# Splitting the second head's weights one stage earlier in a four-layer attention kernel, with the lists of two engines reordered

## What is computed

```python
def _cross_attention(q_in, kv_in, wq, bq, wk, bk, wv, bv, wo, bo, bias_k, bias_v):
    qh = (q_in @ wq + bq).reshape(b, q_len, H, K)      # H, K = 16, 128
    kh = (kv_in @ wk + bk).reshape(b, t, H, K)
    vh = (kv_in @ wv + bv).reshape(b, t, H, K)
    kh = jnp.concatenate([kh, bias_k], axis=1); vh = jnp.concatenate([vh, bias_v], axis=1)
    weights = softmax(einsum('bqhk,bthk->bhqt', qh, kh) / sqrt(K))
    return einsum('bhqt,bthk->bqhk', weights, vh).reshape(b, q_len, H * K) @ wo + bo

x = x + _cross_attention(layer_norm(x, ln1), ctx, ...1)
x = x + _cross_attention(layer_norm(x, ln2), ctx, ...2)
x = x + gelu(layer_norm(x, ln_mlp) @ w_fc1 + b_fc1) @ w_fc2 + b_fc2
```

## Time and profile before

| | |
|---|---|
| median of 3 runs | 1384.41 us (1384.3 to 1389.26) |
| profiled execution | 1390.04 us |
| its span, first to last instruction | 1388.2 us |
| mean granted TensorE clock | 0.93 |
| TensorE busy | 1230.7 us, 89% |
| VectorE, ScalarE, POOL busy | 71%, 52%, 36% |
| opening | 0 to 33.8 us |
| first attention | 33.8 to 353 us |
| norm n02 | 354 to 367 us |
| second attention | 367.6 to 681 us |

### The profile page before, as it was taken

One profiled execution on the slowest core, in us unless ns is written; L12 is line 12 of the kernel. 1 busy time (PEld: TensorE's weight loads), 2 busy tenths in 40 slices (PEclk: granted clock), 3 DMA queues, 4 the chain that ended last, 5 costly groups with the idle time before them and its releaser, 6 DMA issues. The chain is left out here.

```text
span 1388.2 us, 27413 instructions
## 1 busy us (share of the span) xinstructions
PE 1230.7 (89%) x9144; PEld 1014.5 (73%) x9144; DVE 987.8 (71%) x2229; ACT 722.0 (52%) x1636; POOL 495.6 (36%) x642
## 2 busy tenths in 40 slices
PE   5799999999599999999699699969499977699869
PEld 4699999999499999998588455559277756455558
DVE  6478878787578887888763689465488865689464
ACT  4456655666366666566542177441166632177441
POOL 3654545444374445543150000030199940000030
PEclk9899999999799999999899699979799998699979
DMA  4111111010211111010023874020660014874020
GB/s 151 47 31 32 31 30 30 23 30 1 95 32 32 31 31 29 9 38 0 31 65 71 121 83 56 13 77 1 196 131 3 2 51 83 112 81 55 13 65 31
DMA packets 55406, 70.90 MB, mean 51 GB/s; under 512 B 6696, under 2 KB 47404, under 8 KB 52976
## 3 DMA queue, kind: packets, MB, share of 16 engines
q1 hardware_dynamic: 53704, 65.83, 22.8%
q10 hardware_dynamic: 1600, 3.76, 0.9%
HBM read 46.79 MB, written 8.13 MB: 40 GB/s over the span
## 5 line engine op out<-in xcount | busy, mean ns | idle before, releaser
L945 ACT ACTIVATE a_prob<-a_s_ps,a_negmax 128x257 f32<-128x257 f32 x256 | 119.2, 477 | 92.9 <-DVE a_negmax L1027 92.9
L2033 DVE TENSOR_REDUCE s_mx<-s_s_ps 128x2 f32<-128x1024 f32 x128 | 151.9, 1211 | 17.9 <-PE s_s_ps L2078 17.6
L2018 ACT ACTIVATE s_probT<-s_st_ps 128x512 f32<-128x512 f32 x256 | 132.1, 605 | 58.6 <-PE s_st_ps L2092 56.3
L884 POOL TENSOR_TENSOR x_v_hi<-a_v_sum,x_one 128x512 fp32r<-128x512 f32 x60 | 63.2, 1053 | 248.7 <-DVE a_v_sum L1016 248.7
L1822 POOL TENSOR_SCALAR s_below<-s_masked,s_mx 128x256 f32<-128x256 f32 x256 | 117.8, 480 | 30.5 <-DVE s_mx L1850 29.7
L576 POOL TENSOR_TENSOR rstd<-base,power 128x4 f32<-128x4 f32 x4 | 4.0, 1009 | 335.6 <-DVE base L593 335.6
L1042 DVE TENSOR_TENSOR a_pT_lo<-a_t_ps,a_pT_hi 128x512 fp32r<-128x512 f32 x128 | 88.3, 690 | 37.9 <-ACT a_pT_hi L958 36.2
L1027 DVE TENSOR_REDUCE a_negmax<-a_s_ps 128x2 f32<-128x514 f32 x128 | 87.0, 689 | 35.6 <-PE a_s_ps L1088 35.3
L958 ACT ACTIVATE a_pT_hi<-a_t_ps 128x512 fp32r<-128x512 f32 x128 | 76.7, 600 | 59.5 <-PE a_t_ps L1142 56.1
L1850 DVE CUSTOM_DVE_ANT_0 s_masked<-s_s_ps,l_mask 128x256 f32<-128x256 f32 x256 | 90.7, 421 | 16.6 <-PE s_s_ps L1887 16.6
L1835 ACT ACTIVATE s_probT<-s_st_ps 128x512 f32<-128x512 f32 x128 | 69.9, 596 | 29.1 <-PE s_st_ps L1897 29.0
(11 more groups left out here) (289 smaller groups left out, 4069.0 us busy)
## 6 DMA issues: line engine op xcount, KB each, us to landing
a_wo_raw<-L_xattn_wo SPq DMA_DIRECT2D x16, 256.0 KB, 3.2
x_wqk_raw<-L_xattn_wq SPq DMA_DIRECT2D x31, 128.0 KB, 2.3
x_wqk_raw<-L_xattn_wk SPq DMA_DIRECT2D x31, 128.0 KB, 2.3
x_wv_raw<-L_xattn_wv SPq DMA_DIRECT2D x15, 256.0 KB, 3.0
l_k_st<-k_second SPq DMA_DIRECT2D x12, 256.0 KB, 9.6
l_k_st<-k_stack SPq DMA_DIRECT2D x16, 192.0 KB
l_q_st<-q_stack SPq DMA_DIRECT2D x12, 192.0 KB
x_vbias<-L_xattn_bias_v SPq DMA_DIRECT2D x2, 1024.0 KB, 11.0
```

Source lines behind the costliest of these rows:

```text
L945: nc.scalar.activation(prob[:, n % 2, qt, 0:NK], s_ps[:, n % 2, qt, 0:NK], ACT.Exp, bias=negmax[:, n % 2, qt:qt + 1], accum_out=den[:, n % ...
L2018: nc.scalar.activation(probT[:, third % 2, n // 4, n // 2 % 2, n % 2], st_ps[:, u % 3], ACT.Exp, scale=c.scale).then_inc(z.exp_done, 1)
L2033: nc.vector.tensor_reduce(mx[:, i % 2, qt, a::2], s_ps[:, n % 2], AX.X, ALU.max).then_inc(z.max_done, 1)
```

## The change

The second head's `wqk` (slot 1) and the second pair's `wv` are now loaded and split in the stage ahead of each attention: in the opening and in n02. SP loads them there (in the opening once the low parts of the first weights are made, and in front of `prepare_sync`), ScalarE makes the high parts (`split_high`), POOL the low ones (`split_low`). In the attention the first load and split go, the counts that the others wait for are shifted by one, and in the first pair the load of `wv` is left out; the two rows for the next layer are loaded behind `wo`. Apart from that the lists of the opening and of the norms are put into another order; ScalarE norms tiles 4 and 5 too.

```diff
@@ -222,9 +223,8 @@
                                      ALU.subtract, ALU.mult).then_inc(self.z.normed_dve, 1)
 
     def turn(self, pe, half):
-        if half == 0:
-            pe.wait_ge(self.z.normed_act, 2)
-        pe.wait_ge(self.z.normed_dve, (2, 6)[half])
+        pe.wait_ge(self.z.normed_act, 2 * (half + 1))
+        pe.wait_ge(self.z.normed_dve, 2 * (half + 1))
...
@@ -298,6 +296,10 @@
                                  ).then_inc((z.x_in0, z.x_in1)[half], 16)
                 w.load_first_rows(sp, 1, z.vrows_in)
                 sp.dma_start(mask_i[:], ins["mask_BxS2_ik0"]).then_inc(z.mask_in, 16)
+                sp.wait_ge(z.lo_split, 1)
+                w.load_qk(sp, 1, z.second_qk)
+                sp.wait_ge(z.lo_split, 2)
+                w.load_v(sp, 1, z.second_v)
                 w.prepare_sync(sp, z)
                 sp.wait_ge(z.masked, 2)
                 sp.dma_start(core.maskrow, mask_f[:].bitcast(F32)).then_inc(z.mask_out, 16)
@@ -321,23 +323,30 @@
 
                 weights_high(0)
                 context_high(0)
+                context_high(1)
                 weights_high(1)
-                context_high(1)
                 for t in range(2):
                     norm.normalise_scalar(act, t)
                 act.wait_ge(z.cols_in, 16)
                 front.keys_high(act, 0)
+                act.wait_ge(z.second_qk, 32)
+                w.split_high(act, w.second_parts()[0], z.second_hi)
                 front.values_high(act, 0)
+                for t in range(4, 6):
+                    norm.normalise_scalar(act, t)
                 for n in range(2):
                     norm.high(act, n)
                     norm.flat_early(act, n)
                 front.values_high(act, 1)
                 front.keys_high(act, 1)
                 for n in range(2, 4):
-                    norm.high(act, n)
+                    norm.high(act, n, flat=n - 1)
+                front.values_high(act, 2)
                 queries.high(act, 0)
-                front.values_high(act, 2)
                 front.values_high(act, 3)
+                act.wait_ge(z.second_v, 16)
+                front.wait_values(act)
+                w.split_high(act, w.second_parts()[1], z.second_hi)
                 queries.high(act, 1)
 
             @block.gpsimd
...
-                for j in range(4):
+                front.values_low(pool, 0)
+                pool.wait_ge(z.second_hi, 1)
+                w.split_low(pool, w.second_parts()[0], z.second_lo)
+                for j in range(1, 4):
                     front.values_low(pool, j)
+                pool.wait_ge(z.second_hi, 2)
+                w.split_low(pool, w.second_parts()[1], z.second_lo)
 
             @block.tensor
             def _(pe):
...
                 front.keys(pe, 1)
+                front.values(pe, 2)
                 norm.turn(pe, 1)
-                queries.products(pe, 0)
-                for j in range(2, 4):
-                    front.values(pe, j)
-                queries.products(pe, 1)
+                front.values(pe, 3)
+                for g in range(2):
+                    queries.products(pe, g)
 
...
-        names = LayerNorm.SEMS + Queries.SEMS + ("w_in0", "w_in1", "rows_in", "hi_split", "raw_hi")
+        names = LayerNorm.SEMS + Queries.SEMS + ("w_in0", "w_in1", "rows_in", "hi_split", "raw_hi", "second_qk",
+                                                 "second_v", "second_hi", "second_lo")
         z = type("Semaphores", (), {n: st.sem(n) for n in names})
         norm = LayerNorm(st, core, ahead, scale, offset, factor, z)
         queries = Queries(core, ahead, norm.turned, z) if ahead.has_queries else None
         with nc.Block() as block:
             @block.sync
             def _(sp):
+                if queries:
+                    ahead.load_qk(sp, 1, z.second_qk)
+                    ahead.load_v(sp, 1, z.second_v)
                 ahead.prepare_sync(sp, z)
 
             @block.scalar
             def _(act):
                 for t in range(2):
                     norm.normalise_scalar(act, t)
-                for n in range(2):
-                    norm.high(act, n)
-                    norm.flat_early(act, n)
-                if not queries:
+                norm.high(act, 0)
+                norm.flat_early(act, 0)
+                norm.high(act, 1)
+                for t in range(4, 6):
+                    norm.normalise_scalar(act, t)
+                if queries:
+                    act.wait_ge(z.second_qk, 32)
+                    ahead.split_high(act, ahead.second_parts()[0], z.second_hi)
+                else:
                     ahead.prepare_scalar(act, z, range(1))
-                for n in range(2, 4):
-                    norm.high(act, n)
+                norm.high(act, 2)
+                norm.high(act, 3, flat=2)
                 if queries:
+                    act.wait_ge(z.second_v, 16)
+                    ahead.split_high(act, ahead.second_parts()[1], z.second_hi)
                     for g in range(2):
                         queries.high(act, g)
                 else:
@@ -468,12 +493,15 @@
                 core.clear_used(pool)
                 if queries:
                     ahead.first_key_bias(pool, z)
+                    for n, part in enumerate(ahead.second_parts()):
+                        pool.wait_ge(z.second_hi, n + 1)
+                        ahead.split_low(pool, part, z.second_lo)
                 else:
                     ahead.prepare_pool(pool, z)
 
             @block.vector
             def _(dve):
-                norm.shift(dve, 0)
+                norm.shift(dve, 0, 0)
                 for t in range(2, 4):
                     norm.normalise_vector(dve, t)
                 norm.constants(dve)
...
-                dve.wait_ge(z.rstd_done, 1)
-                for t in range(4, TT):
+                norm.low(dve, 0, early=1)
+                norm.shift(dve, 1, 1)
+                for t in range(6, TT):
                     norm.normalise_vector(dve, t)
-                for n in range(2):
-                    norm.low(dve, n)
-                for n in range(2, 4):
-                    norm.flat_after(dve, n)
-                for n in range(2, 4):
-                    norm.low(dve, n)
+                norm.flat_after(dve, 1, high=2)
+                norm.low(dve, 1, late=1)
+                norm.flat_after(dve, 3)
+                norm.flat_after(dve, 2, high=3)
+                norm.low(dve, 2, late=3)
+                norm.low(dve, 3, late=2)
                 if queries:
                     for g in range(2):
                         queries.low(dve, g)
...
+    def second_parts(self):
+
+        return self.qk_parts(1), self.v_parts()
+
+    def split_high(self, act, part, sem):
+        raw, hi, _ = part
+        self.core.nc.scalar.activation(hi, raw, ACT.Copy).then_inc(sem, 1)
+
+    def split_low(self, pool, part, sem):
+        raw, hi, lo = part
+        self.core.nc.gpsimd.tensor_tensor(lo, raw, hi.bitcast(F32), ALU.subtract).then_inc(sem, 1)
...
+        def qk_split(h):
+
+            return 2 * (h - 1)
+
...
@@ -826,24 +878,22 @@
             @block.sync
             def _(sp):
                 def load_qk(h):
-                    wait(sp, z.wqk_split, 2 * (h - 1))
+                    wait(sp, z.wqk_split, qk_split(h - 1))
                     w.load_qk(sp, h, z.wqk_in)
...
-                load_qk(1)
-                if follows:
-                    w.load_first_rows(sp, i + 1, z.next_in)
 
                 def body(p, vs):
                     for s, h, _, fetch in halves(p):
                         if fetch:
                             load_qk(h + 2)
                         if s == 0:
-                            if fetch:
-                                wait(sp, z.wv_split, 2 * p)
+                            if fetch and not first(p):
+                                wait(sp, z.wv_split, wv_split(p))
                                 w.load_v(sp, p + 1, z.wv_in)
                             wait(sp, z.wo_split, 2 * p)
                             sp.dma_start(wo_raw[:], wo[bass.ds(p * PW, PW), :].rearrange("(h p) n -> p h n", p=P)
                                          ).then_inc(z.wo_in, 16)
+                            if follows and first(p):
+                                w.load_first_rows(sp, i + 1, z.next_in)
                 pairs(sp, body)
 
             @block.gpsimd
...
+                    pool.wait_ge(z.wv_in, 16 * (p - 1))
                     wait(pool, z.turn_done, turns.v_out(p - 1))
                     raw, hi, lo = w.v_parts()
                     nc.gpsimd.tensor_tensor(hi, raw, w.times_one(raw.shape[1]), ALU.mult).then_inc(z.wv_split, 1)
-                    pool.wait_ge(z.wv_split, 2 * p - 1)
...
@@ -893,15 +943,13 @@
                                               src[:, bass.ds(h, 1)].bitcast(F32).broadcast_to([P, B])
                                               ).then_inc(z.kbias, 1)
...
```

(8 more changed lines are left out.)

64 lines of the change are left out of this document (33 added, 31 removed).

## The result

The change runs in 1362.99 us (median of 4 runs, 1361.72 to 1364.52), the kernel before in 1384.36 (4 runs, 1379.56 to 1389.26) on the same chip: ratio 0.9847, 95% interval [0.982, 0.9874], 21.4 us less. The forecast was 1360.8, between 1355 and 1371. Two later series of the same file gave 1362.16, ratio 0.9835 [0.9816, 0.9855], and 1362.67, ratio 0.9844 [0.9821, 0.9868].

What follows compares the result with a forecast made beforehand. TensorE, busy 89% of the span, bounds the kernel; only its waits and slow clock at layer edges can be won. Layer one -11.6, layer two -10.5, opening -1.5, norms 0: -23.6 from 1384.4 gives 1360.8 us, range 1355 to 1371.

Steps and rivals of the forecast that it cites:

- The price of the two waits: Attention starts: TensorE's waits for `x_wqk_lo` and `x_wv_lo` plus half clock cost at most 13.1 us (layer one), 11.0 (layer two).
- 0.5 us in each layer for the chain of unit 0: Attention starts: maximum, exponential, normalisation, transposes of unit 0 covered with nothing to spare; 0.5 us kept back per layer.
- 1 us for the clock in layer one: First attention's start: idle TensorE in the opening may drop the clock, costing 0 to 3 us; 1 taken.
- The opening, -1.5: Opening: reordered lists against added splits give -1.5 us, between +1 and -3.5.
- the list by hand (-2.0): Opening: following the lists with the rows' durations, POOL's last subtraction ends latest, at about 31.4, 2.0 us less than before.
- the port: Opening: POOL's two added subtractions could hold up VectorE through the shared port pair, 0 to 2 x 1.1 us; 0.5 taken.
- The norms, 0: Norm between the layers and the one behind: no change, between +1.5 and -1 together; `h_lo` whole at about 364.
- SP's rows in the norm: Norm between layers: rows land at about 366 behind three added loads, stage's last copy at 367.27; covered by 1 us.
- the clock does not come back: Rival: remaining pauses still pull the clock down, only the waits' 16.3 us are returned, 1368 us; chance 0.17.
- The edit does not do what it says: Rival: late second `x_wqk` load holds ScalarE's opening list, each us past 17 moving the opening; 1379 us; chance 0.05.
- The stages ahead pay: Rival: opening and norm end 3 us later each (port, late rows), gain -16 us, 1368 us; chance 0.08.
- The clock sticks low: Rival: half clock persists from a layer's start, 38 us added per pair of heads, 1398 us; chance 0.03.

Runs made afterwards that it cites:

- lists: The change with head two's and value group one's weights loaded and split in the attention as before, only the new list orders kept: 1384.75 us, ratio 1.0006.
- weights: The kernel before with only the early loads and splits of the weights, lists of opening and norms as before: 1363.19 us, ratio 0.9854.
- v_back: The change with the second values group's early load and split put back into the attention, query and key weights still early: 1371.79 us, ratio 0.9904.
- fill_tail: The change with the norms' old lists and 3 + 8 unread extra TensorE products between and behind the opening's query groups: 1358.13 us (one run).
- change_b: The change unaltered, run in the third series beside the second run of the fastest version: 1362.67 us, ratio 0.9844.
- again: The change unaltered, run once more as the measure for its halves: 1362.16 us, ratio 0.9835.
- both: The change with norms' old lists, a POOL wait for VectorE in the opening, extra products at start, opening's tail, norms, 23 before MLP: 1357.19 us, ratio 0.9801.

## Why the prediction was right, and where it was not

- **The price of the two waits.** Right, in size and in mechanism. Taken from the step between score units, it was 13.1 and 11.0 us; where the clock holds, the units take 6.90 or 6.91 us against the 6.83 worked out, and the gain was 13.05 and 10.9. `lists`, `weights` and `v_back` show that it comes from the early weights, and that each of the two has its share. One reading was loose: the clock did not fall behind the wait of 4.9 us but inside it (1.00 in 38 to 39 us, 0.50 in 39.4 to 40.4; the wait ended at 40.38).
- **0.5 us in each layer for the chain of unit 0.** Too much: head 2 is 6.88 to 6.94 in all eleven executions with both weights early. The chain is covered.
- **1 us for the clock in layer one.** Right in its mechanism. It is 1.5 us or nothing from one execution to the next; the row of after shows it (0.50 in 32 to 34 us), and `fill_tail` makes the idle tail its likely cause. Layer one was put at -11.6 and gave -11.55, -13.05 and -11.54. That it met the number so closely is luck: 0.5 us too much for the chain and 0.5 too little for the clock cancel.
- **The opening, -1.5.** -2.9, -1.9 and -2.7 in the three executions of the change: nearer to the list by hand (-2.0), from which I had taken 0.5 back for the port. The port costs 1.07 us in a part of the executions, none in the others, and not where the term had it: VectorE does not meet the added subtractions but the third low part of the values, which the new order brings beside it (in `lists`, with nothing added, POOL took 2.11 us there too). `weights` shows the other half of the step: the early weights alone cost 0.5 us there, the new lists earn 3. POOL's last subtraction was named rightly as what ends last, and ended at 30.52 and 31.53 for the 31.4 by hand.
- **The norms, 0.** This term was mis-sized. "`h_lo` is whole at about 364, as before" overlooked that flat 3 stands ahead of flat 2; it came 0.75 us later. The second norm lost 0.3 to 0.55 more, where its length was to be unchanged. Together +1.1 to +1.3, inside the +1.5 that I had as the bad end. The start of the turn (0.2 us later) was as said.
- **The MLP's start** was not in the sum. It came 1.1 to 1.4 us later in two executions of the change and in `lists`, and not at all in `change_b` and `v_back`, which have the same lists; so the lists are not shown to be its cause. Half clock at its beginning is: behind the first MLP product it lasted 5.4 to 5.9 us in the three executions where the stretch took 49.7 to 49.9, and 2.9 to 3.9 in those where it took 48.5 to 49.0; half of the difference is the loss. With 23 products ahead of it, it was whole and took 1.0 to 1.2 us less than before. Why it lasts longer in some executions stays open.
- **SP's rows in the norm.** By my count they would land 1 us ahead of the stage's end; in the trace SP, when it has them, waits 2.6 us more for the stage to end. Covered with more room.

The rival "the clock does not come back" would have left heads of 11.5 and 10 us; they were 8.4 and 6.9. "The edit does not do what it says" fell with the second `x_wqk` split running at 16.04 us on ScalarE, before the 17 from which on it would have cost. "The stages ahead pay" had both end 3 us later; the opening ended 1.9 to 2.9 us sooner, the norm 0.8 later. "The clock sticks low": in the change the slow stretch left in layer one lasted some 3.4 us.

The sum of the terms was -23.6, and the touched parts gave -22.9; the medians -21.4 to -22.5. What lies between is no more than the scatter of the rest. The sum is better than its terms: the norms and the MLP's start, put at nothing, took 2.4 us, and the opening and layer two gave 1.8 us more than they were put at, which nearly cancels. The two terms that make nine tenths of the sum hold by themselves.

## What to carry to other kernels

A wait inside a loop that is TensorE's costs its length and the slow clock around it. Take its price as the distance between two events of the program around the wait, less the same distance in the unbroken loop: that was good to 0.1 us here where the clock held behind it (in layer one 1.5 us of it stayed in some executions), while the waits' own lengths fall short of it by a third, and in layer two of `v_back` by more than half. Then cut every execution at such events: it shows effects of 0.5 us that the medians, with 9 us of scatter in the untouched rest, do not. And when a list is put into a new order, ask of each instruction which part of its input ends last, and whether it was moved ahead of one that could have run already.

## What the runs showed of the hardware that was not expected

- **Starting first wins one instruction, not a list of them.** Where VectorE subtracts twice and POOL once, POOL issued 0.32 us behind the first, the loser took 0.84 us (POOL) or 1.07 us (VectorE) longer, with one or the other losing in executions of the same file. The Trainium skill (SBUF — State Buffer, "SBUF: two separate sides") says that the port pair that the two share is locked for a whole instruction by the one that starts first, for VectorE among others in an instruction with two inputs in SBUF, as here. The trace agrees for the first subtraction (0.68 us in `again`, 1.75 for the second, which lost); the second may or may not come ahead of the POOL instruction that has been waiting, so a list of several on one engine gives no safe order.
- **Work that nobody needs can shorten a kernel.** `both` has 89 products more than the change (9253 records against 9144, as each of the 20 at the start leaves two) and is 5 to 7 us faster; some 1 us of that is the norms' old lists. The products fell into TensorE's idle time, and the granted clock over the span was 0.951 and 0.952 instead of 0.939 to 0.943. The Trainium skill (TensorE: Matmul & The Clock Gate, "What's actually happening") says that activity is what releases the clock; both the 12 products that ran out too early (first MLP product at 0.77 us) and the 23 that did not (0.47 us) agree. Whether fewer than 23 would do was not tried.
